# Splitting the last FFN tile of a decoder layer over two engines, moving two residual adds, and issuing two of the eight outputs from ScalarE

## The reference, cut to what matters

```python
def act_quant(x):
    scale = 127.0 / jnp.clip(jnp.max(jnp.abs(x), axis=-1, keepdims=True), 1e-05)
    return jnp.clip(jnp.round(x * scale), -128, 127) / scale
...
h = bit_linear(x, w1)                       # 128 -> 512, w1 quantised to -1, 0, 1
h = depthwise_conv1d(h.transpose(0, 2, 1), conv_w, conv_b)   # 3 taps along the tokens
h = jax.nn.silu(h.transpose(0, 2, 1))
return bit_linear(h, w2)                    # 512 -> 128, h quantised per token
...
x = x + _L0_ffn_ref(_layernorm(x, axis=-1), ...)
```

## Time and profile before

| what | us |
|---|---|
| median of 3 runs | 312.63 (312.25 to 312.78) |
| the profiled execution, its own time | 311.38 |
| its span, from the first to the last instruction | 309.6 |
| the same less its span | 1.78 |

### The profile page before, as it was taken

The page is one execution under the profiler, slowest core; times in us unless marked ns, Lnnn a source line. Parts: engine busy times, 40 slices in busy tenths (PEclk is TensorE's granted clock), DMA queues, the critical chain, the costliest instruction groups (busy, mean ns, idle before and its releaser), DMA issues.

```text
span 309.6 us, 6618 instructions
## 1 busy us (share of the span) xinstructions
PE 282.8 (91%) x2446; PEld 179.1 (58%) x2446; DVE 216.5 (70%) x481; ACT 195.3 (63%) x484; POOL 143.8 (46%) x252
## 2 busy tenths in 40 slices
PE   0799699899999989989899999899999999999994
PEld 0567566566666668655566676445454553447763
DVE  3758877886766651778577746987888779447854
ACT  1587477667777770787677731567777767625344
POOL 3704577894577771584446510059119173000331
PEclk9999999999999999999999999999999999999999
DMA  7920000000000000000000000000000000000001
GB/s 279 307 89 3 0 3 1 2 2 0 3 2 3 0 2 0 2 3 0 2 0 2 4 3 0 2 0 0 2 0 1 3 0 3 0 0 2 0 25 44
DMA packets 4835, 6.17 MB, mean 20 GB/s; under 512 B 834, under 2 KB 3650, under 8 KB 4676
## 3 DMA queue, kind: packets, MB, share of 16 engines
q1 hardware_dynamic: 4516, 5.42, 5.0%
q10 hardware_dynamic: 288, 0.33, 0.3%
HBM read 5.23 MB, written 0.52 MB: 19 GB/s over the span
## 4 chain that ended last, share of the span: by engine, by line
PE 73%; DVE 12%; ACT 8%; issue 3%; DMA 2%; SPq 0%; ACTq 0%
PE bank L724 64%; PE bank L797 5%; ACT pr L546 4%; DVE nmax L1370 3%; DVE qk L1415 3%; DMA pT<-in_wv 2%; ACT pT L546 1%; PE bank L949 1%; PE bank L1037 1%; ACT pT L677 1%; DVE pT L1386 1%; DVE stats L1301 1%; DVE xn L1314 0%; DVE onT L1335 0%; DVE km L1324 0%
## 5 line engine op out<-in xcount | busy, mean ns | idle before, releaser
L646 ACT ACTIVATE pT<-bank 128x512 f32<-128x512 f32 (+1 forms) x80 | 44.5, 600 | 25.6 <-PE bank L724 25.1
L339 POOL TENSOR_SCALAR pr<-pr,pinv 128x256 f32<-128x256 f32 (+2 forms) x96 | 45.4, 489 | 28.7 <-DVE pinv L1378 28.6
L1415 DVE TENSOR_REDUCE qk<-bank 128x4 fp32r<-128x616 f32 x64 | 48.9, 795 | 13.6 <-PE bank L724 13.4
L546 ACT ACTIVATE pr<-bank,nmax 128x256 f32<-128x256 f32 (+2 forms) x96 | 44.3, 479 | 18.2 <-DVE nmax L1370 17.9
L724 PE MATMUL bank<-qs 64*128 64x256 f32 (+3 forms) x256 | 49.4, 469 | 4.1 <-ACT pr L546 3.7
L1370 DVE TENSOR_REDUCE nmax<-bank 128x2 f32<-128x512 f32 (+2 forms) x48 | 31.6, 687 | 14.5 <-PE bank L724 14.4
L724 PE MATMUL bank<-pT,v_sb 128*64 128x128 f32 (+2 forms) x320 | 38.4, 385 | 0.0
L339 POOL TENSOR_SCALAR pT<-pT,pinv 128x512 f32<-128x512 f32 x32 | 21.7, 692 | 23.6 <-DVE pinv L1378 23.6
L1386 DVE COPY pT<-bank 128x512 f32<-128x512 f32 (+1 forms) x32 | 30.3, 948 | 1.1 <-PE bank L797 1.1
L724 PEld LDWEIGHTS bank<-pT,v_sb 128*64 128x64 f32 x320 | 21.1, 136 | 14.1 <-issue 10.8
L724 PE MATMUL bank<-km,qk 64*128 64x308 f32 x128 | 27.7, 366 | 1.2 <-DVE qk L1415 1.1
(11 more groups left out here) (190 smaller groups left out, 576.4 us busy)
## 6 DMA issues: line engine op xcount, KB each, us to landing
pT<-in_wqk SPq DMA_DIRECT2D x1, 1024.0 KB, 6.5
cw_sb<-in_cw SPq DMA_DIRECT2D x1, 768.0 KB, 8.2
x_sb<-in_x SPq DMA_DIRECT2D x2, 256.0 KB, 5.6
pT<-in_wv SPq DMA_DIRECT2D x1, 512.0 KB, 7.5
wo_sb<-in_wo SPq DMA_DIRECT2D x1, 512.0 KB, 6.9
out<-x_sb SPq DMA_DIRECT2D x8, 64.0 KB, 1.6
onT<-in_consts ACTq DMA_DIRECT2D x1, 256.0 KB, 6.7
pT<-in_xwk SPq DMA_DIRECT2D x1, 256.0 KB, 7.5
```

The lines of the kernel that those rows point to most:

```text
L339: nc.gpsimd.tensor_scalar(d, d, pinv[:, t, a:a + 1], 1.0, ALU.mult, ALU.mult).then_inc(norm_done, 1)
L546: nc.scalar.activation(prob[r][:, a, at:at + w], bank[:, SP[k % 2] + a, at:at + w], ACT.Exp, bias=nmax[:, t, a:a + 1], accum_out=psum[:, t ...
L646: nc.scalar.activation(px[rows, i, :], bank[rows, (ST0, ST1)[i % 2], :], ACT.Exp, scale=SD ** -0.5).then_inc(xexp_done, 1)
L1415: nc.vector.tensor_reduce(m, s_in, AX.X, ALU.max, negate=True).then_inc(round_done, 1)
```

## The change

Tile 7 is quantised by VectorE in two halves of 256 columns, each with its own count on `hq_last`. TensorE turns each half into a bank of its own (`LAST_TURN`: bank 6 and bank 3). ScalarE copies the first half to `hiT`, VectorE the second (`hiT_last`), and `down_last` waits for one half at a time. On VectorE `finish(3)` no longer stands ahead of `hidden_scale(7)` but behind `quantise_last`, with `finish(4)`; then comes the copy of the half, and then `finish(5)` to `finish(7)`. The factor `hdq` of tile 7 is multiplied on GpSimd. `down(5)`, `down(6)` and `down_last` write into banks of their own (4, 1, 2) and no longer wait for `f_done`. TensorE issues `turn_last(0)` and `turn_last(1)` ahead of `down(6)`. The outputs of tiles 5 and 7 are issued by ScalarE, behind its last copy; SyncE issues the other six.

```diff
--- before.py
+++ after.py
@@ -54,7 +54,8 @@
 VB = (PT, PT + 1, OB)
 CONV_BANK = (PT, PT + 1, SM, SM + 1)
 HIDDEN_BANK = (ST0, ST1)
-DOWN_BANK = (OB, PJ0)
+DOWN_BANK = (OB, PJ0, OB, PJ0, OB, PT + 1, SM, SM + 1)
+LAST_TURN = (ST1, PT)
 OUT_BANK = (ST1, ST0)
 ATT_BANK = (PJ0, OB)
 
@@ -252,8 +253,8 @@
             "xd_done", "xdT_ps", "xdT_done", "conv_ps", "silu_done", "hsc_done", "hiT_ps", "hiT_done", "f_ps",
             "f_done")
         root_done = sem("root_done")
-        pool_chain, qb0_pool, scale_done, hdq_done, hq_last = sem_names(
-            "pool_chain", "qb0_pool", "scale_done", "hdq_done", "hq_last")
+        pool_chain, qb0_pool, scale_done, hdq_done, hq_last, hiT_last = sem_names(
+            "pool_chain", "qb0_pool", "scale_done", "hdq_done", "hq_last", "hiT_last")
 
         block = ctx.enter_context(nc.Block())
         out_t = out.rearrange("b (t p) c -> p (b t) c", p=P)
@@ -280,7 +281,7 @@
 
             sp.wait_ge(km_done, 4 * NG)
             sp.dma_start(cb_sb, cb.to_broadcast([2, FH])).then_inc(ld_cb, 16)
-            for i in range(TT):
+            for i in (0, 1, 2, 3, 4, 6):
 
                 sp.wait_ge(f_done, i + 1)
                 sp.dma_start(out_t[:, i, :], x_sb[:, i, :]).then_inc(st_out, 16)
@@ -492,6 +493,9 @@
             inverse_root(0, 5)
             for i in range(TT - 1):
                 quantise_hidden(i)
+            pool.wait_ge(hsc_done, TT)
+            nc.gpsimd.tensor_scalar(hdq[:, TT - 1:TT], hdq[:, TT - 1:TT], wmean[:, 1:2], 1.0, ALU.mult,
+                                    ALU.mult).then_inc(hdq_done, 1)
 
         @block.scalar
         def _(act):
@@ -715,8 +719,15 @@
                 turned_hidden(i - 2)
             silu(TT - 2)
             silu(TT - 1)
-            for i in range(TT - 4, TT):
+            for i in range(TT - 4, TT - 1):
                 turned_hidden(i)
+            act.wait_ge(hiT_ps, TT)
+            act.wait_ge(f_ps, TT - 2)
+            nc.scalar.activation(hiT[:, 1, 0:FH // 2], bank[:, LAST_TURN[0], 0:FH // 2], ACT.Identity,
+                                 bias=minus_round[:, :]).then_inc(hiT_done, 1)
+            for i in (5, 7):
+                act.wait_ge(f_done, i + 1)
+                act.dma_start(out_t[:, i, :], x_sb[:, i, :]).then_inc(st_out, 16)
 
         @block.tensor
         def _(pe):
@@ -1023,10 +1034,7 @@
 
             def turn_hidden(i):
 
-                if i + 1 < TT:
-                    pe.wait_ge(hq_done, i + 1)
-                else:
-                    pe.wait_ge(hq_last, 1)
+                pe.wait_ge(hq_done, i + 1)
                 if i < 2:
                     pe.wait_ge(xo_done, 2)
                     pe.wait_ge(round_done, rounds[0])
@@ -1038,16 +1046,33 @@
                                                con[:, C_ID:C_ID + P])
                 last.then_inc(hiT_ps, 1)
 
+            def turn_last(h):
+                pe.wait_ge(hq_last, h + 1)
+                if h == 0:
+                    pe.wait_ge(hiT_done, TT - 2)
+                for k in (2 * h, 2 * h + 1):
+                    last = nc.tensor.transpose(bank[:, LAST_TURN[h], k * P:k * P + P], hq[:, 1, k * P:k * P + P],
+                                               con[:, C_ID:C_ID + P])
+                last.then_inc(hiT_ps, 1)
+
+            def down_last():
+                for h in range(2):
+                    pe.wait_ge((hiT_done, hiT_last)[h], (TT, 1)[h])
+                    for k in (2 * h, 2 * h + 1):
+                        last = mm(bank[:, DOWN_BANK[TT - 1], 0:C], hiT[:, 1, k * P:k * P + P], w2_q[:, k, :], k == 0,
+                                  k == FH // P - 1)
+                last.then_inc(f_ps, 1)
+
             def down(i):
                 pe.wait_ge(hiT_done, i + 1)
                 if i == 0:
                     pe.wait_ge(xo_done, 2)
                 elif i == 1:
                     pe.wait_ge(xdTl_done, 3)
-                else:
+                elif i <= 4:
                     pe.wait_ge(f_done, i - 1)
                 for k in range(FH // P):
-                    last = mm(bank[:, DOWN_BANK[i % 2], 0:C], hiT[:, i % 2, k * P:k * P + P], w2_q[:, k, :], k == 0,
+                    last = mm(bank[:, DOWN_BANK[i], 0:C], hiT[:, i % 2, k * P:k * P + P], w2_q[:, k, :], k == 0,
                               k == FH // P - 1)
                 last.then_inc(f_ps, 1)
 
@@ -1279,10 +1304,13 @@
                 down(i - 5)
                 turn_hidden(i - 4)
                 conv(i)
-            for i in range(TT - 4, TT):
+            for i in range(TT - 4, TT - 1):
                 turn_hidden(i)
                 down(i - 1)
-            down(TT - 1)
+            turn_last(0)
+            turn_last(1)
+            down(TT - 2)
+            down_last()
 
         @block.vector
         def _(dve):
@@ -1721,16 +1749,14 @@
                 i, k = TT - 1, slice(TT - 1, TT)
                 dve.wait_ge(hsc_done, TT)
                 dve.wait_ge(hiT_ps, i - 1)
-                nc.vector.tensor_scalar(hq[:, i % 2, :], hs[:, i % 2, :], hscale[:, k], ROUND, ALU.mult,
-                                        ALU.add).then_inc(hq_last, 1)
-                link(nc.vector.tensor_scalar(hdq[:, k], hdq[:, k], wmean[:, 1:2], None, ALU.mult))
-                settle()
+                for cols in (slice(0, FH // 2), slice(FH // 2, FH)):
+                    nc.vector.tensor_scalar(hq[:, i % 2, cols], hs[:, i % 2, cols], hscale[:, k], ROUND, ALU.mult,
+                                            ALU.add).then_inc(hq_last, 1)
 
             def finish(i):
-                if i + 1 < TT:
-                    dve.wait_ge(hdq_done, i + 1)
+                dve.wait_ge(hdq_done, i + 1)
                 dve.wait_ge(f_ps, i + 1)
-                nc.vector.scalar_tensor_tensor(x_sb[:, i, :], bank[:, DOWN_BANK[i % 2], 0:C], hdq[:, i:i + 1],
+                nc.vector.scalar_tensor_tensor(x_sb[:, i, :], bank[:, DOWN_BANK[i], 0:C], hdq[:, i:i + 1],
                                                x_sb[:, i, :], ALU.mult, ALU.add).then_inc(f_done, 1)
 
             hidden_scale(0)
@@ -1744,10 +1770,17 @@
             hidden_scale(2)
             hidden_scale(3)
             for i in range(4, TT):
-                finish(i - 4)
+                if i < TT - 1:
+                    finish(i - 4)
                 hidden_scale(i)
             quantise_last()
-            for i in range(TT - 4, TT):
+            finish(TT - 5)
+            finish(TT - 4)
+            dve.wait_ge(hiT_ps, TT + 1)
+            dve.wait_ge(f_ps, TT - 2)
+            nc.vector.tensor_scalar(hiT[:, 1, FH // 2:FH], bank[:, LAST_TURN[1], FH // 2:FH], -ROUND, None,
+                                    ALU.add).then_inc(hiT_last, 1)
+            for i in range(TT - 3, TT):
                 finish(i)
 
 
```

## The result

The changed kernel takes 311.26 us (median of 22 runs, 310.18 to 312.21) and the kernel before, in 22 runs beside it, 312.14 (310.53 to 313.66). The ratio is 0.997, with a 95% interval of 0.9956 to 0.9983: 0.3% faster. The median fell by 0.88 us; 0.8 was forecast. (The forecast 311.8 lies 0.5 higher, since it starts from 312.63, the median of three runs, and not from 312.14.) The profiled execution took 311.60 us, with a span of 309.7.

A forecast was written before the change was run, and what follows sets the result against it. One compute thread through tile 7 up to 306.84 us, then 2.3 us of output, were taken to bound the end. Compute -0.85 with an unchanged 2.3 us output, rounded to -0.8, gave 312.63 - 0.8 = 311.8 us, range 310.9 to 312.9.

The forecast's parts named there:

- Compute part: Tile 7's chain from silu to last residual: the residual ends at 305.99 instead of 306.84, -0.85 us.
- maximum: Tile 7's row maximum on VectorE starts at 302.61, 0.37 us earlier, with `finish(3)` moved behind the quantisation.
- two halves: VectorE's quantisation of tile 7: two passes of 0.35 us overlapping by 0.09, ending at 304.06 and 304.32.
- ScalarE's half: ScalarE's copy of 256 turned PSUM columns of tile 7: 0.469 us, from 304.70 to 305.17.
- `finish(7)` right behind `finish(6)`: VectorE is the late one next: the last residual would be ready at 305.56 and starts at 305.64.
- the term of the transposes: TensorE's turning of tile 7: two take 0.38 us, the second pair starts 0.04 after its half, ending at 304.74.
- `hdq` on GpSimd: Tile 7's factor step of 0.26 us beside a 1.9 us path, charged at nothing.
- Rival 3: Smaller compute gain: VectorE's second half waits for GpSimd, or residuals do not overlap; some -0.5, 312.1; chance 0.09.
- Output part: Tile 7's output keeps 2.3 us as the transfer moves with TensorE's end; landing at 308.3, 0.85 off the end.
- rival 1: Output no longer disturbed: tile 7's own queue spares its long issue, landing 1.5 after issue; -1.65, 311.0; chance 0.13.
- The rule quoted from the Trainium skill: Outputs: the queue move is worth at most 0.78 us, and nothing if the blocked engine decides.
- The base: Difference worked out in one profiled execution (311.38 us, tile 7 landing at 309.17) and taken off the 312.63 median.

The follow-up runs named there:

- outs_all_sp: The changed kernel with all eight outputs issued by SyncE; 311.80 us, ratio 0.9993 to the kernel before.
- before_again: The kernel before, unedited, profiled once more; no instruction transfer among its outputs, 6.84 us from tile 7's silu to the end.
- pad_after: The changed kernel with 24 tiny matmuls ahead of TensorE's first transpose, moving its later instructions by 48 places; 310.64 us, ratio 0.9953.
- after_again: The changed kernel, unedited, profiled once more; span 309.2 us.
- queue_only: The kernel before with only the outputs of tiles 5 and 7 issued by ScalarE, behind its last copy; 311.75 us, ratio 0.9994.
- tail_act: The changed kernel with the outputs of tiles 4 to 7 issued by ScalarE, 0 to 3 by SyncE; 311.48 us, ratio 0.9985.
- the two padded kernels: The kernel before and the changed one, each with 24 tiny matmuls ahead of TensorE's first transpose; 311.28 and 310.64 us.

## Why the prediction was right or wrong

**Compute part: right, 0.85 forecast, 0.74 measured.** Point by point: maximum at +0.63 (forecast 0.37 earlier than +1.00, the same); two halves in 0.63 (0.61); ScalarE's half in 0.47 and VectorE's in 0.42 (0.469, 0.425); `finish(7)` right behind `finish(6)` on VectorE, as the one that is late next. The missing 0.11 is in the term of the transposes: they ended at +2.86, against 304.74 - 301.98 = 2.76, because the second half ended 0.03 later than reckoned (+2.37) and the second pair closed 0.49 behind it, not 0.04 + 0.38. VectorE's copy waited for it (+2.90 against +2.80). By the runs the gain divides into 0.35 for `finish(3)`, 0.14 for the split quantisation, 0.20 for the second copier and 0.10 for `hdq`, measured one at a time against the full change. The sum, 0.79, is close to 0.74. Such figures need not add up, and the banks of their own and the order of `turn_last` ahead of `down(6)` were not tested by themselves.

**`hdq` on GpSimd: charged at nothing, and rightly for the path.** But the overlap in the earlier trace rows was too short to show what happens: GpSimd's step stretched from 0.26 to 0.42 beside VectorE's halves and to 0.53 beside the single pass, with over 1.4 us to spare before `finish(7)` needs it. For tile 6 in the kernel before it ran wholly beside a `tensor_reduce` of VectorE (303.22 to 303.49, against 302.98 to 303.66) and took its usual 0.27. In its direction that agrees with the exclusion which the Trainium skill states ("SBUF — State Buffer", Who interferes with whom), with GpSimd as the one that waits; it waited 0.16 and 0.27 us, less than the 0.35 and 0.48 of VectorE's passes. That a port is the cause was not tested otherwise. Rival 3's version, in which VectorE waits, didn't occur beyond 0.06.

**Output part: the number right by luck, the step wrong.** I had the last landing at 308.3 - 301.98 = +6.32; it was +6.31. But the step said that tile 7 keeps its 2.3 us because the transfer moves along with TensorE's end. In fact the transfer came 1.35 us earlier than in the one profile I had, not 0.85, and in other executions of the kernel before it comes after all outputs; tile 7's issue took 0.42 and its landing 1.9; and tile 6, stuck behind tile 4 on SyncE, was last. I took up rival 1's thought that a queue of its own spares tile 7 the stall, which happened, and missed that SyncE's queue would stall elsewhere. The rule quoted from the Trainium skill ("DMA: Bandwidth & Descriptors", Issuing engines are not separate DMA queues), that a second issuer saves only issue time, agrees: outs_all_sp lost its 0.55 us in waiting issues, while each of the last three outputs landed 1.6 us after its issue.

**The base: the step that was not seen.** "The profiled execution" of the kernel before was one with a disturbed output. before_again reaches its end 0.76 us earlier with identical computing. Against it the changed kernel gains next to nothing at the end: its last output lands at +6.31 in one profile and at +6.43 in the other, where before_again's lands at +6.39. So the 0.8 us that I took off was reckoned against a disturbed end, which not every timed run of the kernel before has; how many have it isn't known. With the transfer out of the way on both sides the medians differ by 0.64, which is not clear of noise from 0.88. The timed runs can be sorted by TensorE's mean granted clock, which takes out the loss near 40 us (59 runs of the kernel before, taken beside the experiments, 22 of the changed one, 12 of pad_after):

| runs at a clock of 0.998 or more | runs | span, median | lowest | highest |
|---|---|---|---|---|
| before | 22 | 309.7 | 308.6 | 311.3 |
| changed | 8 | 308.4 | 308.3 | 308.7 |
| pad_after | 3 | 308.0 | 307.9 | 308.1 |

The lowest spans differ by 0.3 us, the medians by 1.3. The kernel before runs much longer than its best more often than the changed one, but the 308.7 is not a firm upper end: after_again, the changed kernel's other execution at full clock, had a span of 309.2. The output can spread the kernel before by 0.8 us (its two profiles), which doesn't cover 308.6 to 311.3. Part of the rest lies at the start: ScalarE's first pass of line 546 (550 in the changed kernel) starts at 18.71 us in before_again, at 19.04 in queue_only and at 19.14 in after_again, all three at full clock, and at 17.51 in tail_act, and this lead or lag lasts to tile 7's silu but for the clock's loss. None of these kernels differs from the one before so early. What sets the start stays open. So does what makes the last transfer of the old tail come now at +4.35 and now at +7.8.

## What to carry to other kernels

Follow a shortened end through to the landing of each output: here 0.74 us of computing was gained, and the order in which outputs meet a late instruction transfer decided nearly as much: 0.56 us between the changed kernel and pad_after, 0.8 between the kernel before and itself. Two versions are best compared where neither meets the transfer, as in the two padded kernels. Before taking a tail's cost from one profile, take a second one of the same kernel and look at whether an issue is unusually long. If an instruction transfer lies among the last outputs, moving TensorE's instructions by some tens of places in an idle stretch can be worth nearly as much as a rewritten tail (0.56 us by the last landing here, against 0.63), and outputs that follow each other closely do better on two queues.

## What the runs showed of the hardware that I had not expected

- One instruction transfer of 0.9 to 1.4 us, a single packet, holds up an output issue made during it when the previous output of the same queue has not landed: issues of 1.11 to 1.73 us on SyncE (seven profiles) and 0.83 on ScalarE, where 0.33 to 0.45 is usual. They end some 0.4 us after the transfer. Outputs under way at that time took up to 2.9 us to land, where 1.5 to 1.6 is usual.
- Where that transfer falls differs between executions of one kernel: about +4.35 once and +7.8 once for the kernel before.
- A 0.26 us step of GpSimd on one column took 0.42 to 0.53 us beside a VectorE `tensor_scalar` within SBUF, and 0.27 beside a `tensor_reduce`.
- Fourteen profiles of kernels that are the same up to the FFN, but for the padding, spread by 1.6 us at ScalarE's first softmax pass, near 18 us.
